# First stage of a one-core decoder-layer kernel: value chunks added on VectorE before the sum, three gates in front of it, weight splits placed elsewhere

## The reference, cut to what matters

```python
x1  = ln(x, ln1_g, ln1_b);  xln = ln(x1, tm_g, tm_b);  xs = shift(xln)
mix = xln * time_first + xs * (1 - time_first)
v   = xln @ Wv
r   = sigmoid(mix @ Wr)                                  # the gate
dec = exp(time_decay * (T - 1 - arange(T))[:, None])
vmix = einsum('bth,th->bh', v, dec)                      # one row of 512
x2  = x + r * (vmix @ Wo + bo)                           # the same row for every token
xc  = ln(ln(x2, ln2_g, ln2_b), cm_g, cm_b);  xcs = shift(xc)
out = x2 + sigmoid(xc @ Wcr) * (square(relu(xcs @ Wck)) @ Wcv)   # channel mix
```

## Time and profile before

| | |
|---|---|
| median of 3 runs | 1094.7 us (1092.39 to 1098.47) |
| the profiled execution's own time | 1089.49 us |
| its span, first to last instruction | 1087.5 us |
| PE busy | 1050.0 us, 97% of the span |
| DVE busy | 574.4 us, 53% |
| ACT busy | 536.5 us, 49% |
| POOL busy | 431.9 us, 40% |

### The profile page before, as it was taken

One profiled execution on the slowest core, in us unless ns is written; L12 is line 12 of the kernel. 1 busy time (PEld: TensorE's weight loads), 2 busy tenths in 40 slices (PEclk: granted clock), 3 DMA queues, 4 the chain that ended last, 5 costly groups with the idle time before them and its releaser, 6 DMA issues.

```text
span 1087.5 us, 17100 instructions
## 1 busy us (share of the span) xinstructions
PE 1050.0 (97%) x4892; PEld 844.3 (78%) x4893; DVE 574.4 (53%) x1110; ACT 536.5 (49%) x892; POOL 431.9 (40%) x327
## 2 busy tenths in 40 slices
PE   2999999999999999999999999999999999999998
PEld 0446878888788878887887878888888888888887
DVE  7977855925390548050007497945445544454514
ACT  4634626333433333333334343357777766776742
POOL 1012303320222132211223423377777777887641
PEclk9899999999999999999999999999999999999999
DMA  8705168525532642234253891067999999987678
GB/s 282 261 1 193 58 235 307 175 78 191 177 97 78 221 164 89 88 132 155 97 206 132 302 300 58 5 196 162 280 192 259 230 234 313 208 192 140 89 175 343
DMA packets 98306, 192.91 MB, mean 177 GB/s; under 512 B 13000, under 2 KB 33480, under 8 KB 97744
## 3 DMA queue, kind: packets, MB, share of 16 engines
q1 hardware_dynamic: 79008, 151.63, 40.0%
q0 software_dynamic: 18816, 39.87, 19.4%
q10 hardware_dynamic: 432, 0.79, 0.2%
HBM read 137.78 MB, written 60.03 MB: 182 GB/s over the span
## 4 chain that ended last, share of the span: by engine, by line
PE 77%; DVE 10%; DMA 7%; issue 3%; ACT 1%; SPq 1%; POOL 1%; ACTq 0%; DVEq 0%; POOLq 0%
PE bank L613 36%; PE bank L937 21%; PE bank L1541 10%; PE bank L525 3%; DMA shx_d<-yo,idy 3%; PE bank L1533 2%; DMA res_d<-yo,idy 2%; PE bank L1549 1%; DMA hT_d<-hT 1%; DVE big L1326 1%; SPq L1060 1%; DVE mx L359 1%; DMA g1b<-in_L_attn_ln_b 1%; PE bank L948 1%; DVE bns L248 1%
## 5 line engine op out<-in xcount | busy, mean ns | idle before, releaser
L918 POOL TENSOR_TENSOR ksp_lo<-ra,ksp_hi 128x512 fp32r<-128x512 f32 x96 | 145.8, 1519 | 447.1 <-ACT ksp_hi L868 447.0
L1685 DVE TENSOR_TENSOR wds<-w,wds 128x1024 fp32r<-128x1024 f32 x84 | 103.1, 1228 | 158.8 <-ACT wds L1622 158.8
L1541 PE MATMUL bank<-w,xT 128*128 x672 | 158.8, 379 | 1.2 <-ACT xT L1606 0.8
L937 PE MATMUL bank<-vring,ksp_hi 128*128 128x512 f32 x512 | 159.4, 393 | 0.0
L860 ACT ACTIVATE ra<-bank 128x512 f32<-128x512 f32 x96 | 57.4, 598 | 177.2 <-PE bank L613 174.9
L1541 PEld LDWEIGHTS bank<-w,xT 128*128 128x128 f32 x672 | 126.9, 189 | 21.6 <-issue 1.8
L613 PE MATMUL bank<-wds,aT 128*128 128x512 f32 x504 | 137.3, 407 | 0.0
L868 ACT ACTIVATE ksp_hi<-ra 128x512 fp32r<-128x512 f32 x96 | 60.7, 632 | 124.7 <-PE bank L937 124.3
L937 PEld LDWEIGHTS bank<-vring,ksp_hi 128*128 128x128 f32 x512 | 95.5, 188 | 20.0
L613 PE MATMUL bank<-xcT_hi,wck_lo 128*128 128x512 f32 x256 | 101.7, 397 | 0.0
L613 PE MATMUL bank<-xcT_lo,wck_hi 128*128 128x512 f32 x256 | 101.5, 396 | 0.0
(11 more groups left out here) (267 smaller groups left out, 1920.6 us busy)
## 6 DMA issues: line engine op xcount, KB each, us to landing
vring<-wcv_d SPq DMA_DIRECT2D x64, 512.0 KB, 3.3
w<-in_L_ffn_Wu SPq DMA_DIRECT2D x32, 512.0 KB, 7.5
w<-in_L_ffn_Wd SPq DMA_DIRECT2D x32, 512.0 KB, 8.9
hT_d<-hT SPq DMA_DIRECT2D x16, 512.0 KB, 3.7
hTb<-hT_d SPq DMA_DIRECT2D x3, 2048.0 KB, 10.9
raw_wcv<-in_L_attn_Wcv SPq DMA_DIRECT2D x4, 1024.0 KB, 6.6
raw_wck<-in_L_attn_Wck SPq DMA_DIRECT2D x4, 1024.0 KB, 9.5
f<-in_L_attn_x SPq DMA_DIRECT2D x4, 1024.0 KB, 6.9
```

The source lines that it names most:

```text
L918: nc.gpsimd.tensor_tensor(ksp[1][:, i % 2], ra[:, i % 2], ksp[0][:, i % 2], ALU.subtract).then_inc(sem("klo_in"), 1)
L937: m = nc.tensor.matmul(bank[to + j][:], ksp[l][:, i % 2, j * P:(j + 1) * P], rhs(r), start=i == 0 and k == 0, stop=i == last and k == 2)
L1541: m = nc.tensor.matmul(bank[4 + u][:, 0:EI], xT4[:, u, c * P:(c + 1) * P], slot_of(wu8[:, :, c * EI:(c + 1) * EI], e), start=c == 0, stop= ...
L1685: nc.vector.tensor_tensor(wds[:, u, 1], slot_of(wd8, e), wds[:, u, 0], ALU.subtract).then_inc(sem("wl4"), 1)
```

## The change

Six things change, all in the first stage and at its seam with the second.

1. DVE adds the four chunks of `pv` (two adds, then one), and `pe_vmix` has 4 matmuls in place of 16. It waits for the last add (`pv_sum`).
2. PE has the gates of the tiles 0, 1 and 2 ahead of `pe_vmix`, and `pe_row` directly behind it. Before, one gate stood ahead, one between, and two behind.
3. On DVE the low part of `wcv0` stands ahead of `dve_mix` of block 1. The low part of `wck0` goes from behind `pv` to behind the low parts of the transposes, and `dve_front_x` goes ahead of the four `vmb`.
4. On ACT `wcr` is split where `wck0` was. A sigmoid of four unused numbers stands ahead of the first gate, so that the table load that sigmoid needs comes there. `wck0` is split between two gates of block 1. `SPLIT_ORDER` follows.
5. The transposes of block 0 for the channel mix stand behind the third gate of block 3, on PE and on ACT. Before, they stood behind the second.
6. Stage 2 no longer waits for `wck0` at its head but at the first use of it.

```diff
-        SPLIT_ORDER = ("wr", "wcv0", "wck0", "wcr", "wcv1", "wcv2", "wck1", "wck2", "wck3", "wcv3")
+        SPLIT_ORDER = ("wr", "wcv0", "wcr", "wcv1", "wck0", "wcv2", "wck1", "wck2", "wck3", "wcv3")
...
             dve_lo(dve, "wr")
+            dve_lo(dve, "wcv0")
             dve_mix(dve, 1)
-            dve_lo(dve, "wcv0")
...
                 nc.vector.scalar_tensor_tensor(out=pv[:, c], in0=bank[c][:], scalar=tm_g[:, c:c + 1], in1=wv[:, c],
                                                op0=ALU.mult, op1=ALU.mult).then_inc(sem("pv_in"), 1)
-            dve_lo(dve, "wck0")
+            dve.wait_ge(sem("pv_in"), C)
+            for c in (0, 2):
+                nc.vector.tensor_tensor(pv[:, c], pv[:, c], pv[:, c + 1], ALU.add).then_inc(sem("pv_sum"), 1)
+            dve.wait_ge(sem("pv_sum"), 2)
+            nc.vector.tensor_tensor(pv[:, 0], pv[:, 0], pv[:, 2], ALU.add).then_inc(sem("pv_sum"), 1)
+            front = dve_front_x(dve, 0, tmp0)
             dve.wait_ge(sem("dwb_in"), 1)
             for c in range(C):
                 dve.wait_ge(sem("vm_in"), c + 1)
                 nc.vector.tensor_scalar(vmb[:, c], bank[c][:, 0:P], dwb[:, c:c + 1], None,
                                         ALU.add).then_inc(sem("vmb_in"), 1)
-            front = dve_front_x(dve, 0, tmp0)
...
             act_norm(act, 4)
-            act_hi(act, "wck0")
+            act_hi(act, "wcr")
             act_turned(act, 1)
-            act_hi(act, "wcr")
+            nc.scalar.activation(vm[:], vm[:], ACT.Sigmoid).then_inc(sem("table_in"), 1)
...
             act_gate(act, 1, 2)
+            act_hi(act, "wck0")
             act_gate(act, 1, 3)
...
-            for j in (0, 1):
+            for j in (0, 1, 2):
                 act_gate(act, 3, j)
             act.wait_ge(sem("gwf_in"), 16)
             nc.scalar.activation(gw[0][:], gwf[:], ACT.Copy).then_inc(sem("gwhi"), 1)
             act_hi_xc(act, 0, first=True)
-            for j in (2, 3):
-                act_gate(act, 3, j)
+            act_gate(act, 3, 3)
...
-            pe.wait_ge(sem("pv_in"), C)
+            pe.wait_ge(sem("pv_sum"), 3)
             for h in range(C):
-                for c in range(C):
-                    i = nc.tensor.matmul(bank[h][:, 0:P], pv[:, c, h * P:(h + 1) * P], onesq[:],
-                                         start=c == 0, stop=c == C - 1)
+                i = nc.tensor.matmul(bank[h][:, 0:P], pv[:, 0, h * P:(h + 1) * P], onesq[:], start=True, stop=True)
                 i.then_inc(sem("vm_in"), 1)
...
-            pe_gate(pe, 0, 0)
+            pe_gate(pe, 0, 0, 1, 2)
             pe_vmix(pe)
-            pe_gate(pe, 0, 1)
             pe_row(pe)
-            pe_gate(pe, 0, 2, 3)
+            pe_gate(pe, 0, 3)
...
-            pe_gate(pe, 3, 0, 1)
+            pe_gate(pe, 3, 0, 1, 2)
             pe.wait_ge(sem("mix_in"), NB * C)
             for c in range(C):
                 pe_turn_xc(pe, 0, c)
-            pe_gate(pe, 3, 2, 3)
+            pe_gate(pe, 3, 3)
...
             dve_lo_xc(dve, 0, first=True)
+            dve_lo(dve, "wck0")
...
-                if first and i and i % 4 == 0:
+                if first and i % 4 == 0:
                     pe.wait_ge(sem("wlo"), split_count(f"wck{i // 4}"))
...
-            pe.wait_ge(sem("wlo"), max(split_count("wcr"), split_count("wck0")))
+            pe.wait_ge(sem("wlo"), split_count("wcr"))
```

## The result

The changed kernel takes 1084.12 us (median of 7 runs, 1081.86 to 1089.09), beside 1091.69 us for the kernel before (median of 7). The ratio is 0.9919, with a 95% interval of 0.9895 to 0.9943: faster, by under 1.1%. A later series gave 0.9936 (0.9914 to 0.9957).

What follows compares the result with a forecast made beforehand. PE was taken to bound the kernel, with 77% of the chain. Savings of 6.1 (first stretch) and 2.1 (seam) sum to 8.2 us, so 1094.7 − 8.2 = 1086.5 us, range 1080.5 to 1092.5.

Steps and rivals of the forecast that it cites:

- First stretch: PE from gate 0 to the transposes of block 2: 22.47 us would become 16.3, saving 6.1.
- the sum 0.9: PE's sum over the partitions, cut to 4 matmuls, would take 0.9 us instead of 5.23.
- the wait for `vmb` 0.45: New PE wait between sum and product with `Wo`: 0.35 for the last `vmb`, 0.1 for two hand-overs.
- The seam: PE's wait for `tmp` at the transposes goes, saving 2.1 us; covers 0.8 for `tmp`, 0.5 for the low parts.
- The edits at nothing: Covered adds, `wck0` and `wcr` splits, table load and earlier `wcv0` store would cost PE 0 us.
- A loss of 2.7: If the earlier `wcv0` store slowed the reload of x, `dve_front_x` would delay PE 2.7 us; counted as nothing.
- Rival A: PE's clock falls at the new wait behind the sum, losing 1.5 to 3 us; time 1088.8, chance 0.12.
- Rival B: DVE comes 0.8 or more late at the seam, PE waits, up to 2.1 us lost; 1088.6, chance 0.15 with E.
- D: Slower: routed experts lose 0.23 us or more per tile; at 0.3 the time is 1104, chance 0.03.
- E: In the first stretch `pv` or its adds come after 98.5, needing 3.2 us more on DVE; counted with B, 0.15.
- Rival C: Routed experts under full DMA engines give back 5 us, leaving a gain of 3; time 1091.7, chance 0.10.
- sign of being wrong: The prediction is wrong if stage 2 opens 8 us earlier and the kernel's end does not.

Runs made afterwards that it cites:

- the split ahead: Kernel before with only the low part of `wcv0` moved on DVE ahead of the mix of block 1; ratios to before 1.0000 and, run again, 0.9953.
- before again: The kernel before, unchanged, profiled a second time; interval from gate 0 to the product with `Wcr` 61.55 us, ratio to before 1.0013.
- the one with the late table load: Changed kernel without the early sigmoid of four unused numbers, so the table load stands between `pv` and the first gate on ACT; ratio to before 0.9918.

## Why the prediction was right, point by point

- **First stretch, 6.1 us.** It came out at 5.9 (22.47 − 16.56) against the trace that the forecast was read from, and at 4.3 (20.84 − 16.56) against the second trace of before, in which the clock did not fall. The order, the wait that went and the one that came were as worked out. Two terms were too small: the sum 0.9 for a measured 1.05, and the wait for `vmb` 0.45 for 0.62. I had priced one `vmb`, but with four matmuls in 1.05 us DVE gets them nearly together: it starts the first at 97.62 and ends the fourth at 98.75. The new first stretch is 16.56, where 16.3 was forecast. (By its starts the product with `Wo` is 3.03 and the gate behind it 3.13, where the prediction has 3.31 and 2.79. Their sum is nearly the same.)
- **The seam, 2.1 us.** From the transposes of block 2 to the product with `Wcr` 40.71 became 38.42, so 2.3. The covers were thinner than worked out and held: `tmp` was ready at 138.37 for PE's 139.01 (0.6, forecast 0.8), the low parts at 143.1 for 143.50 (0.4, forecast 0.5). Putting the old seam back into the changed kernel brought the wait back (2.12).
- **The edits at nothing.** The adds took 2.0 us with 3.0 of cover. The reload of x landed at most 8.5 after its issue where 7.7 was the earlier trace rows, with the store of `wcv0` right behind it, and DVE never waited for it. A loss of 2.7 was not there. Two transfers of one queue overlapped here, and the earlier one lost 0.8: in all nine traces with the early store its longest was 8.4 to 8.6, in the four without 7.4 to 7.7. The Trainium skill ("DMA: Bandwidth & Descriptors", Queues, rings and completion order) says that each DMA engine takes one ring's descriptors in order. By that rule the reload keeps its 7.7. The traces agree in the main and differ from it by 0.8.
- **Rival A** (the clock falls at the new wait) did not come. In five traces with a wait of 0.4 to 0.6 for `vmb` the sum and the product stayed at full clock.
- **Rival B** did not come, in any trace with the new seam. D and E did not come either: the last add ended 3.0 us ahead of PE, and the changed kernel is faster in both series.
- **Rival C** (given back in the experts) is what the first trace seems to show, with 7.5 us more there. It is not the change's. The kernels with the old first stage had 318.8 to 325.4 in six traces, and those with the changed one, or one edit off it, 320.4 to 327.7 in seven. Their means are 322.9 and 323.2, worked out from the table. Nor is it given back between the interval and the experts, where the means are 567.4 and 566.7. The spread of 9 us goes with one wait, whatever the first stage: PE's waits for `a` of DVE in the experts add up to 1.3 us in the trace with 318.8, to 1.9 with 320.2, to 4.1 and 4.2 with 325.4 and 325.3, and to 6.1 with 327.7. The waits themselves are about half of the spread. Why they differ between executions was not looked for. So the prediction's own sign of being wrong, an end that does not move, showed in the first trace and was this scatter: the second trace of changed has the same interval and ends 8.4 before the second of before.
- **What was right by luck.** The sum took off 1.6 us for the half clock behind the wait for `pv` as if it were always there, and nothing for the clock at the seam. In the second trace of before the clock fell at neither. In four other traces, all of edited kernels, it fell at the old seam, which costs 1.6 there. So the saving is 6.6 us in waits and matmuls (61.55 − 54.98) and 1.6 for each fall that a run of before has. How many it has is open. Its own two traces have one fall in four waits, half a fall a run, which gives 7.4. The five falls in eight waits of all kernels give 1.25 a run and 8.6, but count kernels in which the seam may behave otherwise. The times, 8.8 and 7.0, allow either and also 6.6. The interval met the 8.2 because the trace that the forecast was read from had exactly one.

## What to carry to other kernels

A sum on another engine's operands is worth moving only when the mover is covered: the same three adds were worth 2.6 us behind three gates and nothing without them. Where one engine bounds, place work in front of the narrow neck and not behind it, and work out for every seam by how much each input is early: at the new seam covers of 0.3 to 0.6 us held in all seven traces. Taking 2 us of wait away gave 3.6 in one pair of traces, so read the granted clock behind it. And compare a stretch that the edit can reach, from one start to another: in the changed kernel it repeated to 0.02 us, and in the kernel before it differed by one fall of the clock, while the ends of two traces of one kernel lay up to 8.5 us apart (1085.3 and 1093.8, the split ahead).

## What the runs showed of the hardware that was not expected

- Whether TensorE's clock falls behind a wait of 2.0 to 2.3 us is not fixed by the wait. In these traces it fell behind 5 of 8 such waits in the two places (before: yes at `pv`, no at the seam; before again: no and no; the four other old seams: yes). A wait of 3.37 was followed by full clock and one of 4.26 by half clock. Each of the five falls cost 1.6 us, the one behind 4.26 cost 2.5. What decides it was not found. At the old seam it fell in all four traces of edited kernels and in neither of before, so it is not ruled out that the edits have a part in it.
- PE waited for the routing on DVE for 1.4 to 2.6 us in most traces and not at all in two (the first of before and the one with the late table load), with the same instructions there. So two executions can differ by some 2 us from this place alone. The cause was not looked for.
